# A rebuilt beginning with 40 identity matmuls on TensorE, up to the second tile's key and query transposes

## Time and profile before

| | us |
|---|---|
| median of three runs | 475.66 |
| the profiled execution, its own time | 477.61 |
| its span, first to last instruction | 475.7 |
| TensorE busy | 444.3 (93%) |
| VectorE busy | 389.0 (82%) |
| ScalarE busy | 286.7 (60%) |
| GpSimd busy | 182.8 (38%) |
| mean granted TensorE clock | 0.985 |

### The profile page before, as it was taken

How to read it: one execution, slowest core, us unless ns; L and a number is a source line. 1 busy time by engine, 2 the same in 40 slices (tenths; PEclk the granted TensorE clock), 3 DMA queues, 4 the chain that set the end, 5 groups by cost and what they waited for, 6 DMA issues and landing times.

```text
span 475.7 us, 12795 instructions
## 1 busy us (share of the span) xinstructions
PE 444.3 (93%) x4816; PEld 382.1 (80%) x4816; DVE 389.0 (82%) x857; ACT 286.7 (60%) x553; POOL 182.8 (38%) x322
## 2 busy tenths in 40 slices
PE   0679999999999999999999999999999999999996
PEld 0557787878887778878888988988988988988985
DVE  6689888898889877977977977977977877887775
ACT  3457777778888666365466466457457447447443
POOL 4479998379996332114112112112112112202100
PEclk9979999999999799999999999999999999999999
DMA  8930000000003000223213223312312312312330
GB/s 231 271 152 23 3 3 23 1 4 1 3 1 72 3 2 1 52 56 83 68 52 84 68 55 77 77 50 72 83 50 66 88 50 61 99 44 55 99 92 22
DMA packets 27815, 28.54 MB, mean 60 GB/s; under 512 B 10960, under 2 KB 19072, under 8 KB 27520
## 3 DMA queue, kind: packets, MB, share of 16 engines
q1 hardware_dynamic: 27392, 27.48, 22.1%
q10 hardware_dynamic: 384, 0.52, 0.5%
HBM read 9.11 MB, written 2.10 MB: 24 GB/s over the span
## 4 chain that ended last, share of the span: by engine, by line
PE 74%; DVE 14%; POOL 4%; SPq 3%; DMA 2%; issue 2%; ACT 1%; ACTq 0%; DVEq 0%; POOLq 0%
PE bank L1025 13%; PE bank L1027 12%; PE bank L1026 12%; PE bank L1241 10%; PE bank L1121 6%; PE bank L1263 6%; PE bank L1104 3%; PE bank L1085 3%; PE bank L1142 2%; SPq L293 2%; DVE kT L758 2%; DMA xa<-in_x 2%; DVE pT L904 2%; DVE on L777 1%; DVE pb L932 1%
## 5 line engine op out<-in xcount | busy, mean ns | idle before, releaser
L904 DVE STREAM_TRANSPOSE pT<-eb 128x512 f32<-128x512 f32 x64 | 44.5, 700 | 38.3 <-ACT eb L618 35.0
L1241 PE MATMUL bank<-w_raw,eb 128*128 128x130 f32 x512 | 60.8, 276 | 1.3 <-DVE w_raw L895 1.3
L1241 PEld LDWEIGHTS bank<-w_raw,eb 128*128 128x128 f32 x512 | 58.5, 190 | 2.7 <-DVE w_raw L895 2.3
L629 ACT ACTIVATE pb<-pb 128x768 f32<-128x768 f32 (+1 forms) x48 | 37.2, 774 | 28.2 <-DVE pb L932 28.2
L1025 PE MATMUL bank<-mun_h,xlT_l 128*128 128x512 f32 x128 | 52.1, 407 | 0.0
L932 DVE TENSOR_TENSOR pb<-bank,rh 128x384 f32<-128x384 f32 x96 | 49.3, 513 | 3.3
L624 ACT CAST xlT_h<-bank 128x256 fp32r<-128x256 f32 x16 | 5.9, 372 | 76.1 <-PE bank L1213 76.1
L618 ACT ACTIVATE eb<-bank,nshift,rn 128x512 f32<-128x512 f32 x64 | 46.2, 776 | 7.8 <-PE bank L1027 7.6
L1027 PE MATMUL bank<-mun_h,xlT_h 128*128 128x512 f32 x128 | 50.5, 395 | 0.0
L545 ACT COPY pT<-bank 128x512 f32<-128x512 f32 x64 | 37.6, 588 | 21.3 <-PE bank L1104 20.5
L1026 PE MATMUL bank<-mun_l,xlT_h 128*128 128x512 f32 x128 | 50.5, 394 | 0.0
(11 more groups left out here) (159 smaller groups left out, 1155.4 us busy)
## 6 DMA issues: line engine op xcount, KB each, us to landing
mu_raw<-pT SPq DMA_DIRECT2D x248, 64.0 KB, 2.0
mu_raw<-in_L_ffn_mu SPq DMA_DIRECT2D x1, 2048.0 KB, 10.1
out<-w_raw SPq DMA_DIRECT2D x16, 128.0 KB, 1.9
xa<-in_x SPq DMA_DIRECT2D x1, 1536.0 KB, 8.5
w_raw<-in_L_ffn_W SPq DMA_DIRECT2D x2, 512.0 KB, 10.1
w_raw<-in_L_ffn_W SPq DMA_DIRECT2D x1, 1024.0 KB, 7.3
xa<-in_x SPq DMA_DIRECT2D x1, 512.0 KB, 3.5
ctile<-in_ctx SPq DMA_DIRECT2D x1, 512.0 KB, 5.2
```

The source lines that it names most:

```text
L904: v.transpose(eblk[:, :, 4 * c:4 * c + 4, :].rearrange("p m e j -> p e m j"), eb[:, 4 * c:4 * c + 4, :].rearrange("p e (m j) -> p e m j", ...
L1241: m = mm(bank[HB[i]][:, n * 2 * HC:(n + 1) * 2 * HC], eb[:, e, :], xw[:, e, :], start=True, stop=True)
```

## The change

- The loads are reordered: context of tiles 0 and 1 first and of 2 to 7 behind the positions; Wq and Wkv are issued by ScalarE; `scale` and `bout` go later. W1's two parts and W2 get a semaphore each.
- GpSimd clears `vw` in VectorE's place, makes neither xn(0), xn(1) nor the rope sums of tiles 0 and 1, splits W1 in step 0 and before, and W2 in steps 5 and 6; `clear_xw` goes from step 5 to step 7; the deviations of tiles 4 to 15 go into step 1 behind `rope_sums(2)`.
- ScalarE runs one small sine at its beginning; `v_copy(0)` goes behind `k1_copy(0)`, and `q_copy(0)` to VectorE.
- VectorE makes `hmask` at its beginning, splits the weights ahead of xn(0) and xn(1), which it now makes, then the angles with `xT_low(0)` among them, and both rope sums of tiles 0 and 1. The statistics of tiles 4 to 9 go to the end of step 0, those of tiles 10 to 15 and the moments into step 1. `rope_products(1)` goes behind the first subtraction of step 0.
- TensorE runs `project_qk(1)` and `project_v(0)` behind `logits(0)`, and gets 22 + 5 + 6 + 3 + 4 matmuls of the identity by itself (128x128 each), into banks 0 and 5, whose results nobody reads: ahead of `transpose_x(0)`, ahead of `project_qk(0)`, ahead of `transpose_kq(0)`, ahead of step 0, and in step 0 ahead of `transpose_kq(1)`.

The diff without its context lines and blank lines:

```diff
@@ -130,13 +130,13 @@
-        w12_loaded = sem("w12_loaded")
+        w12_loaded = [sem("w1a_loaded"), sem("w1b_loaded"), sem("w2_loaded")]
-        ctx_loaded = [sem("ctx_loaded0"), sem("ctx_loaded1"), sem("ctx_loaded2")]
+        ctx_loaded = [sem("ctx_loaded0"), sem("ctx_loaded1"), sem("ctx_loaded2"), sem("ctx_loaded3")]
-        consts_dve = sem("consts_dve")
+        vw_step = sem("vw_step")
@@ -173,6 +173,7 @@
+        k1_filled = sem("k1_filled")
@@ -297,22 +298,21 @@
-            load_ctx(0, 0, 8)
+            load_ctx(0, 0, 2)
-            sp.dma_start(wqkv_raw[:, 0:KD, :], Wq.rearrange("(k p) n -> p k n", p=P)).then_inc(wqkv_loaded, 16)
-            sp.dma_start(wqkv_raw[:, KD:KD + 2, :], Wkv.rearrange("p (k n) -> p k n", k=2)).then_inc(wqkv_loaded, 16)
+            load_ctx(1, 2, 8)
-            sp.dma_start(scaleb[:], row(scale, 1)).then_inc(small_loaded, 16)
-            sp.dma_start(boutb[:], row(bout, DIM)).then_inc(bout_loaded, 16)
-                             W1[:, k * P:(k + 1) * P, :].rearrange("e p h -> p e h")).then_inc(w12_loaded, 16)
+                             W1[:, k * P:(k + 1) * P, :].rearrange("e p h -> p e h")).then_inc(w12_loaded[k], 16)
+            sp.dma_start(boutb[:], row(bout, DIM)).then_inc(bout_loaded, 16)
-                         W2.rearrange("e h d -> (e h) d").rearrange("(k p) d -> p k d", p=P)).then_inc(w12_loaded, 16)
+                         W2.rearrange("e h d -> (e h) d").rearrange("(k p) d -> p k d", p=P)).then_inc(w12_loaded[2], 16)
+            sp.dma_start(scaleb[:], row(scale, 1)).then_inc(small_loaded, 16)
-            load_ctx(1, 8, 12)
-            load_ctx(2, 12, 16)
+            load_ctx(2, 8, 12)
+            load_ctx(3, 12, 16)
@@ -343,6 +343,12 @@
+            g.memset(vw[:].rearrange("p a b c d -> p (a b c d)"), 0.0).then_inc(vw_step, 1)
+            pool.wait_ge(vw_step, 1)
+            for j in range(2):
+                g.memset(vw[64 * j:64 * j + 64].rearrange("p a b c d -> p (a b c) d")[:, :, j * VC + HD], 1.0)\
+                    .then_inc(vw_step, 1)
+            pool.wait_ge(vw_step, 3)
@@ -394,8 +400,8 @@
-                if j == 0:
-                    pool.wait_ge(w12_loaded, 48)
+                if j in (0, 2, 4):
+                    pool.wait_ge(w12_loaded[j // 2], 16)
@@ -436,8 +442,12 @@
-                if s + 1 < TILES:
+                if 0 < s and s + 1 < TILES:
+                if s == 1:
+                    pool.wait_ge(var1_ready, 2)
+                    deviations(ln1, AHEAD, TILES, r1_step, 5, r1_ready)
+                    pool.wait_ge(r1_ready, 2)
@@ -447,24 +457,21 @@
-            norm_x(0)
-            norm_x(1)
-            rope_sums(0)
+            pool.wait_ge(xn_ready, 2)
+            split_w(0)
+            split_w(1)
-            step(0, (split_w, (0,)), (split_w, (1,)))
-            pool.wait_ge(var1_ready, 2)
-            deviations(ln1, AHEAD, TILES, r1_step, 5, r1_ready)
-            pool.wait_ge(r1_ready, 2)
-            step(1, (split_w, (2,)), (split_w, (3,)), (square_mu, (0,)))
-            step(2, (square_mu, (1,)), (split_w, (4,)))
-            step(3, (square_mu, (2,)), (split_w, (5,)))
-            step(4, (square_mu, (3,)), (split_w, (6,)))
-            step(5, (split_w, (7,)), (clear_xw, ()))
-            step(6)
-            step(7, (mu_norms, ()))
+            step(0, (split_w, (2,)), (split_w, (3,)))
+            step(1, (square_mu, (0,)))
+            step(2, (square_mu, (1,)))
+            step(3, (square_mu, (2,)))
+            step(4, (square_mu, (3,)))
+            step(5, (split_w, (4,)), (split_w, (5,)))
+            step(6, (split_w, (6,)), (split_w, (7,)))
+            step(7, (mu_norms, ()), (clear_xw, ()))
@@ -527,10 +534,12 @@
+            act.dma_start(wqkv_raw[:, 0:KD, :], Wq.rearrange("(k p) n -> p k n", p=P)).then_inc(wqkv_loaded, 16)
+            act.dma_start(wqkv_raw[:, KD:KD + 2, :], Wkv.rearrange("p (k n) -> p k n", k=2)).then_inc(wqkv_loaded, 16)
+            act.wait_ge(consts_pool, 2)
+            a.activation(warm[:], mhalf[:, 0:1], ACT.Sin).then_inc(warmed, 1)
-            act.wait_ge(ang_ready, 1)
-            a.activation(ang[:], ang[:], ACT.Sin).then_inc(sin_ready, 1)
@@ -652,13 +661,16 @@
-            act.wait_ge(consts_dve, 3)
+            act.wait_ge(vw_step, 3)
-            v_copy(0)
+            act.wait_ge(ang_ready, 1)
+            a.activation(ang[:], ang[:], ACT.Sin).then_inc(sin_ready, 1)
-            q_copy(0)
+            act.wait_ge(k1_filled, 1)
+            v_copy(0)
+            act.wait_ge(warmed, 1)
@@ -684,11 +696,10 @@
-            v.memset(vw[:].rearrange("p a b c d -> p (a b c d)"), 0.0).then_inc(consts_dve, 1)
-            dve.wait_ge(consts_dve, 1)
-            for j in range(2):
-                v.memset(vw[64 * j:64 * j + 64].rearrange("p a b c d -> p (a b c) d")[:, :, j * VC + HD], 1.0)\
-                    .then_inc(consts_dve, 1)
+            dve.wait_ge(consts_pool, 4)
+            v.reduce_sum(hmask_g[:], ident[:].rearrange("p (n d) -> p n d", d=HD), AX.X).then_inc(hmask_step, 1)
+            dve.wait_ge(hmask_step, 1)
+            v.reduce_sum(hmask[:], hmask_g[:].rearrange("p (g j) -> p j g", j=4), AX.X).then_inc(hmask_step, 1)
@@ -715,6 +726,24 @@
+            def norm_x(t):
+                v.tensor_scalar(xn[:, t, :], xa[:, t, :], ln1[:, 4, t].unsqueeze(1), ln1[:, 6, t].unsqueeze(1),
+                                ALU.subtract, ALU.mult).then_inc(xn_ready, 1)
+            def xT_low(t):
+                dve.wait_ge(xT_split, t + 1)
+                v.tensor_tensor(flat(xT[1][:, t % 2]), bank[7][:, 0:3 * P], flat(xT[0][:, t % 2]).bitcast(F32), ALU.subtract)\
+                    .then_inc(xT_ready, 1)
+            dve.wait_ge(wqkv_step, 1)
+            v.tensor_tensor(flat(wqkv[1]), flat(wqkv_raw), flat(wqkv[0]).bitcast(F32), ALU.subtract)\
+                .then_inc(wqkv_ready, 1)
+            dve.wait_ge(r1_ready, 1)
+            norm_x(0)
+            norm_x(1)
@@ -728,6 +757,7 @@
+            xT_low(0)
@@ -738,11 +768,6 @@
-            def xT_low(t):
-                dve.wait_ge(xT_split, t + 1)
-                v.tensor_tensor(flat(xT[1][:, t % 2]), bank[7][:, 0:3 * P], flat(xT[0][:, t % 2]).bitcast(F32), ALU.subtract)\
-                    .then_inc(xT_ready, 1)
@@ -793,10 +818,15 @@
-                if s + 1 < TILES:
+                if 0 < s and s + 1 < TILES:
+                if s == 0:
+                    rope_products(1)
+                    rope_sums(1)
+                if s == 1:
+                    stats1(AHEAD + 6, TILES)
@@ -804,6 +834,9 @@
+                if s == 1:
+                    dve.wait_ge(st1_ready, TILES)
+                    moments(st1, ln1, AHEAD, TILES, 1.0, LN_EPS, var1_step, 7, var1_ready)
@@ -816,6 +849,9 @@
+                if s == 0:
+                    dve.wait_ge(x_loaded[1], 16)
+                    stats1(AHEAD, AHEAD + 6)
@@ -837,10 +873,20 @@
-            dve.wait_ge(wqkv_step, 1)
-            v.tensor_tensor(flat(wqkv[1]), flat(wqkv_raw), flat(wqkv[0]).bitcast(F32), ALU.subtract)\
-                .then_inc(wqkv_ready, 1)
-            xT_low(0)
+            def rope_sums(t):
+                dve.wait_ge(ropeab_done, t * 2 + 2)
+                wait(dve, q_filled, t)
+                for e in range(2):
+                    v.tensor_tensor(qkr[:].rearrange("p a (n e) -> p (a n) e", e=2)[:, :, e],
+                                    ra[:].rearrange("p h (c e) -> p (h c) e", e=2)[:, :, e],
+                                    rb[:].rearrange("p h (c e) -> p (h c) e", e=2)[:, :, 1 - e],
+                                    ALU.add).then_inc(qk_roped, 1)
+            def q_copy(t):
+                dve.wait_ge(q_filled, t + 1)
+                v.tensor_copy(qT[:], bank[6][:, DIM:2 * DIM].rearrange("p (j n) -> p j n", j=2)).then_inc(q_ready, 1)
@@ -849,27 +895,19 @@
-            dve.wait_ge(x_loaded[1], 16)
-            for t in range(AHEAD, AHEAD + 6):
-                v.bn_stats(st1[:, t, :], xa[:, t, :]).then_inc(st1_ready, 1)
+            rope_sums(0)
-            dve.wait_ge(consts_pool, 4)
-            v.reduce_sum(hmask_g[:], ident[:].rearrange("p (n d) -> p n d", d=HD), AX.X).then_inc(hmask_step, 1)
-            dve.wait_ge(hmask_step, 1)
-            v.reduce_sum(hmask[:], hmask_g[:].rearrange("p (g j) -> p j g", j=4), AX.X).then_inc(hmask_step, 1)
-            for t in range(AHEAD + 6, TILES):
-                v.bn_stats(st1[:, t, :], xa[:, t, :]).then_inc(st1_ready, 1)
-                if t == AHEAD + 8:
-                    dve.wait_ge(hmask_step, 2)
-                    k_copy(0)
+            k_copy(0)
+            q_copy(0)
+            def stats1(t0, t1):
+                for t in range(t0, t1):
+                    v.bn_stats(st1[:, t, :], xa[:, t, :]).then_inc(st1_ready, 1)
-                if s == 1:
-                    dve.wait_ge(st1_ready, TILES)
-                    moments(st1, ln1, AHEAD, TILES, 1.0, LN_EPS, var1_step, 7, var1_ready)
@@ -1029,7 +1067,7 @@
```

(22 more changed lines are left out.)

## The result

The changed kernel took 480.99 us (median of 479.83, 480.64, 481.33 and one disturbed execution of 1493.98 that counts in no comparison; without it the median is 480.64), the kernel before 475.61 (475.06 to 476.0, four executions). The ratio is 1.0106, 95% interval [1.0082, 1.0129]: slower, by 5 us. The forecast of 475.5 with a range to 478.2 was wrong.

What follows compares the result with a forecast made beforehand. VectorE's held queue bounds the beginning, TensorE with VectorE step 3 onward; logits(3)'s start decides the end. 4.4 us gained before logits(0), 4.2 given back by step 3: 475.5 us, own range 474.7 to 476.7, 8-in-10 range 472.8 to 478.2.

Steps and rivals of the forecast that it cites:

- first x held by Wq and Wkv: Beginning: weights loaded from ScalarE's queue beside the first x delay it by 0.6 us, bounds 0 to 1.5.
- deviations beside the weights' split: Before xn(0): VectorE's weight split meets GpSimd's deviations at the SBUF port, 0.9 us lost, bounds 0 to 1.2.
- products wait for a projection at 1.2 GHz: Before tile 0's rope products: projection hidden beside VectorE; at 1.2 GHz logits(0) would come 0.5 us later.
- rope sums: Before logits(0): tile 0's two sums on VectorE take 0.4 us each, where GpSimd takes 1.65.
- steps 0 to 2: From logits(0) to logits(3): 35.2 us, against 31.03 before.
- the start of logits(0): First part of the forecast: logits(0) starts at 19.0 us instead of 23.44, 4.4 earlier.
- The debt of the moved statistics: Steps 0 to 2: statistics and moments moved there, with GpSimd's queue behind, give back 4.2 of 4.4 us by step 3.
- the slower side: Steps 2 to 6: TensorE's clock falls once more, costing 2.3 us, end at 477.8; slower in all 0.28.
- upper terms of the start together: Beginning: load and port terms both at their upper ends, 1.5 and 1.2 us, put the end at 476.7.
- the matmuls don't lift the clock, +0.5: Beginning: identity matmuls fail to raise TensorE's clock, +0.5 us at most, 476.0, within the forecast.
- The faster side's case: Step 13: 2.3 us of its 13.0 may be absent, end at 473.2; faster cases together 0.36.

Runs made afterwards that it cites:

- e9_split_waits: Changed kernel with GpSimd's first split of W1 waiting until VectorE's rope sums of tile 0 are done; ratio 1.0031 to the kernel before.
- e5_stats_undo: Changed kernel with the twelve moved statistics and their moments back at their old places; ratio 1.0015 to the kernel before.
- e3_w_behind_x: Changed kernel with Wq and Wkv issued on SyncE's queue right behind the first x; 475.49 us, ratio 0.9980 to the kernel before.
- e14_e3_stats_undo: Changed kernel with Wq and Wkv behind the first x and the twelve statistics and moments at their old places; ratio 1.0009 to the kernel before.
- both repeats: The changed kernel measured twice more, unedited; 478.56 and 479.46 us, ratios 1.0049 and 1.0058 to the kernel before.
- e7_stats_in_gap: e3_w_behind_x with four statistics in VectorE's wait for logits(0), six at the end of step 0, two in step 1; ratio 0.9955 to the kernel before.
- e4_busy34: Changed kernel with 34 identity matmuls instead of 22 ahead of transpose_x(0); ratio 1.0041 to the kernel before.
- e1_again: The changed kernel unedited, first repeat; 478.56 us, ratio 1.0049 to the kernel before.
- e2_no_busy: Changed kernel without any of the 40 identity matmuls; 483.22 us, ratio 1.0140 to the kernel before.
- e13_again: The changed kernel unedited, second repeat; 479.46 us, ratio 1.0058 to the kernel before.
- e10_stats_early: e3_w_behind_x with angles before the weights' split, five statistics in VectorE's wait for logits(0), seven and moments ending step 0; 473.58 us, ratio 0.9958.

## Why the prediction was wrong

The bound was read rightly: from step 3 on nothing changed, and the start of logits(3) decided the end. Term by term, up to logits(0):

| term | forecast | measured |
|---|---|---|
| first x held by Wq and Wkv | 0.6 (0 to 1.5) | 1.3 |
| deviations beside the weights' split | 0.9 (0 to 1.2) | 0.9 |
| products wait for a projection at 1.2 GHz | 0 (0.5 at most) | 0.8 (0 in `e9_split_waits`) |
| rope sums | 0.8 in all | 1.9 |
| logits(0) | 19.0 | 21.4 |
| steps 0 to 2 | 35.2 | 35.5 |

**The step that failed is the start of logits(0)**, and in it three terms: 0.7 + 0.8 + 1.1 = 2.6, less 0.2 in the small pieces. With these costs in the place of the statistics, what I had counted among the largest gains, their absence ahead of the products, was worth 0.2 us at logits(0) (`e5_stats_undo`).

*The load.* I took a value near the lower bound because the second transfer is issued later. The trace moved the first statistic by 1.32 us, near the 1.45 that the DMA engines' 362 GB/s gave in the earlier trace rows, and `e3_w_behind_x` took it away again. This is what the Trainium skill, DMA: Bandwidth & Descriptors, section Issuing engines are not separate DMA queues, would have given: transfers of different issuers share the same engines and interleave. The trace agrees with it. Bound and rule pointed to the same end, and I chose against both.

*The rope sums.* I moved them from GpSimd to VectorE at 0.4 each and asked only for their own cost. But I had noted, further on, that "W1 is split in waits of GpSimd before step 1". Those waits are just where VectorE does the sums, with both inputs in SBUF. A price of such a meeting, 0.9 us, was in the trace of before, though with GpSimd as the one that was held. That each term had been weighed alone was the mistake; `e9_split_waits` shows the 1.1 us. For the deviations I did see the same collision and sized it rightly: 1.90 us instead of the 1.03 to 1.09 without it. The Trainium skill, SBUF — State Buffer, section Who interferes with whom, has the first to issue hold the port for its whole instruction. The trace agrees where VectorE is first, in the form that GpSimd waits for the rest: the split ran from 8.18 to 9.41, GpSimd's instruction began at 8.39 and took 0.87 longer. Where GpSimd was first, in `e14_e3_stats_undo`, it does not: the two ran side by side and the split kept its 1.23. So the size was right, but the term was a race of 0.1 to 0.2 us, which I had not seen.

*The clock.* I had the identity matmuls end between 6.7 and 11.6 and reckoned that "only about 0.5 us stands on the path". They took 7.32 us, between my 4.9 and 9.8, and ended at 9.09, 2.9 us before TensorE's next work, since xn(0) had come late through the held load and the port. The three errors are thus linked, as far as the traces tell: the later the projection, the later the sums, and the more of them fell beside GpSimd's split. `e3_w_behind_x` shows it the other way, 1.35 us of load being worth 3.2 at logits(0) in its trace. The clock's part is the loose one. It fell at the projection in both repeats too, behind pauses of TensorE of 2.9, 3.3 and 3.1 us, and in `e7_stats_in_gap` behind one of 2.2; it held behind 0.2 us (`e4_busy34`), 1.5 us (`e3_w_behind_x`) and also 2.6 us (`e9_split_waits`). So the longer pauses go with the fall, with one exception; that they cause it is likely and not shown.

**What was right.** The debt of the moved statistics (35.2 against 35.5, and 31.5 with them back), and the path that I had for it: counted from logits(0), GpSimd's deviations began at +19.9 (forecast 19.6) and `transpose_kq(3)` at +30.5 (30.2), and from there it was 5.0 to logits(3). Nothing came from the splits of W2, and no step behind logits(3) changed but for the usual variation. Inside step 0 the agreement is partly luck. The sums of tile 1 took 1.84 us there beside another split, where I had 0.8, and the chain of waits ran not through VectorE's queue but through ScalarE's `v_copy(0)` and table load (24.2 to 26.7) and TensorE at 1.2 GHz (30.2 to 33.6). In `e1_again`, with the clock low elsewhere, steps 0 to 2 took 36.3.

**The rivals.** I had the slower side as one more fall of the clock in steps 2 to 6 (477.8). The changed kernel is slower by about that amount, but for another reason. Its upper terms of the start together (476.7) came nearer to the mechanism and still left out the sums. The case "the matmuls don't lift the clock, +0.5" was off too: without them the kernel is 4.7 us slower (`e2_no_busy`), as far as its trace shows through steps 0 to 2 and not the beginning. The faster side's case that step 13 may lose its 2.3 us came true in `e13_again` (10.5 us) and not in the first trace (13.0).

**What stays open.** Why the clock falls in one execution in step 0 and in the next in step 1 and 2 isn't told by any trace here, nor why it holds in some executions through the projection. Nor is it shown how much of the difference between `e10_stats_early` and the kernel before is the earlier logits(0) and how much step 13, which took 10.5 us in that profile and 13.0 before.

## What to carry to other kernels

When work moves to another engine, price it beside what the other engines do in that very stretch, not by its own length: a sum that costs 0.38 us alone cost 0.95 beside a GpSimd split. In a beginning bound by loads, put transfers on one queue in the order in which they are needed: weights issued beside the first load from a second queue held it by 1.3 us, and 3.1 us of the median hung on it. Work taken out of the beginning is not free later, where every engine's queue is full; look for a wait that is long enough (here VectorE's own wait for the first logits, although these runs don't tell its gain from none) before moving it. And read a term off more than one trace: with the same program up to there, logits(0) came at 18.2 us in one execution and at 20.5 in another.

## What the runs showed of the hardware that I had not expected

Forty matmuls whose results nobody reads were worth 4.7 us in one kernel and 1.4 in another, by the medians. In the trace of the first none of it lay before logits(0), and 2.7 us lay in steps 0 to 2; in that of the second 1.2 us lay before logits(0).

Whether a VectorE instruction with two inputs in SBUF holds a GpSimd one depended here on 0.1 us of order: GpSimd's took 1.83 to 2.00 us when it began 0.11 to 0.28 behind VectorE's, and 1.03 when it began 0.06 ahead of it, and then VectorE's was no longer either.

The granted clock falls at different places in executions of the same kernel. Step 13 took 13.0 us before and after, 11.5 in `e1_again`, 10.5 in `e13_again` and `e3_w_behind_x`. Over 21 to 35 executions the kernel before ranged over 3.2 to 4.3 us, so the interval of a comparison of three and four executions was too narrow, or the sessions differ: neither repeat lies in it.
